# Attention scores of one 256-row batch element: one block-diagonal product per tile before, one product per head after

## The reference, cut to what matters

```
x = x + tanh(g_xattn) * xattn(layernorm(x), ctx)
x = x + tanh(g_ffn)   * ffn(layernorm(x))

xattn:  q = rms_norm(q_in @ Wq per head, qn_w)      # 4 heads of 64
        k = rms_norm((ctx @ Wkv)[k part] per head, kn_w);  v = the other part
        scores = einsum('bqhd,bkhd->bhqk', q, k) / 8       # 256 x 77 for each head
        out = softmax(scores) @ v;  out @ Wfc + fc_b
ffn:    top 2 of 8 experts per row, softmax of the two logits, capacity 97 of a batch element's 256 x 2 places,
        sum over the two kept experts of weight * (x @ We[e])
```

## Time and profile before

| | |
|---|---|
| median of three runs | 1390.62 us |
| profiled execution, first to last instruction (span) | 1388.5 us |
| TensorE matmuls busy | 1364.6 us, 98% of the span |
| TensorE weight loads busy | 1137.0 us, 82% |
| VectorE busy | 1046.5 us, 75% |
| ScalarE busy | 913.9 us, 66% |
| GpSimd busy | 775.2 us, 56% |

### The profile page before, as it was taken

The page is one execution under the profiler, slowest core; times in us unless marked ns, Lnnn a source line. Parts: engine busy times, 40 slices in busy tenths (PEclk is TensorE's granted clock), DMA queues, the critical chain, the costliest instruction groups (busy, mean ns, idle before and its releaser), DMA issues. The chain is left out here.

```text
span 1388.5 us, 26883 instructions
## 1 busy us (share of the span) xinstructions
PE 1364.6 (98%) x8116; PEld 1137.0 (82%) x8116; DVE 1046.5 (75%) x3057; ACT 913.9 (66%) x2600; POOL 775.2 (56%) x947
## 2 busy tenths in 40 slices
PE   7899999999999999999999999999999999999998
PEld 6688888888888888888888888888888888888876
DVE  6877877777877777877778777778777788777763
ACT  6776666775666766667766667666677666676652
POOL 4355555656555656555555566565555555555644
PEclk9999999999999999999999999999999999999999
DMA  5001101011111011110111010111110110101000
GB/s 164 30 18 46 45 28 45 18 45 45 37 37 45 18 46 45 32 42 25 38 45 45 29 45 18 45 45 36 38 39 24 45 45 31 43 18 46 25 16 23
DMA packets 70289, 53.72 MB, mean 39 GB/s; under 512 B 45888, under 2 KB 53504, under 8 KB 70144
## 3 DMA queue, kind: packets, MB, share of 16 engines
q1 hardware_dynamic: 70144, 52.00, 12.1%
HBM read 25.11 MB, written 16.78 MB: 30 GB/s over the span
## 5 line engine op out<-in xcount | busy, mean ns | idle before, releaser
L332 PE MATMUL bkM<-we,x2T 128*128 128x512 f32 x3072 | 791.7, 400 | 0.8 <-DVE acc_v L1067 0.7
L332 PEld LDWEIGHTS bkM<-we,x2T 128*128 128x128 f32 x3072 | 553.6, 188 | 127.6 <-ACT a_out L684 8.4
L684 ACT ACTIVATE a_out<-bkM,gate 128x256 f32<-128x256 f32 x512 | 217.0, 482 | 161.1 <-PE bkM L332 159.9
L1067 DVE SCALAR_TENSOR_TENSOR acc_v<-bkM,gate,acc_v 128x256 f32<-128x256 f32 x384 | 184.8, 481 | 106.2 <-PE bkM L332 91.3
L498 POOL TENSOR_TENSOR a_sum<-a_sum,a_out 128x256 f32<-128x256 f32 x256 | 188.9, 738 | 56.8 <-ACT a_out L684 20.5
L485 POOL TENSOR_TENSOR probs<-probs,p_inv 128x308 f32<-128x308 f32 x128 | 89.8, 702 | 211.6 <-DVE p_inv L960 211.6
L453 POOL TENSOR_TENSOR rstd<-ve,minus_half 128x4 f32<-128x4 f32 x64 | 65.2, 1019 | 145.6 <-DVE ve L872 145.4
L453 POOL TENSOR_TENSOR q_r<-q_ve,minus_half 128x8 f32<-128x8 f32 x64 | 105.0, 1642 | 48.6 <-DVE q_ve L945 48.6
L590 ACT ACTIVATE xn<-x_sb,shift,rstd 128x256 f32<-128x256 f32 x128 | 66.5, 590 | 92.4 <-DVE shift L881 92.4
L453 POOL TENSOR_TENSOR k_r<-k_ve,minus_half 77x8 f32<-77x8 f32 x32 | 52.4, 1637 | 126.9 <-DVE k_ve L921 126.9
L503 POOL TENSOR_TENSOR y<-a_sum,acc_v 128x256 f32<-128x256 f32 x128 | 94.4, 738 | 17.3 <-issue 0.4
(11 more groups left out here) (178 smaller groups left out, 2714.7 us busy)
## 6 DMA issues: line engine op xcount, KB each, us to landing
x_sb<-in_x SPq DMA_DIRECT2D x32, 512.0 KB, 3.7
out<-y SPq DMA_DIRECT2D x64, 256.0 KB, 2.0
ctx_sb<-in_ctx SPq DMA_DIRECT2D x32, 154.0 KB
vf<-v_nat SPq DMA_DIRECT2D x64, 77.0 KB
stage<-in_L_ffn_We SPq DMA_DIRECT2D x2, 1024.0 KB, 7.1
vf<-v_nat SPq DMA_DIRECT2D x32, 52.0 KB
vf<-v_nat SPq DMA_DIRECT2D x32, 51.0 KB
vf<-v_nat SPq DMA_DIRECT2D x32, 26.0 KB
```

The costliest lines, as they stand in the source:

```text
L332: mm = nc.tensor.matmul(out, l, r, start=(i == 0), stop=(i == len(terms) - 1))
L684: ins = nc.scalar.activation(a_out[:, t % 2, (e // 4) * 2 + i], bkM[1][:, i * D:(i + 1) * D], ACT.Copy, scale=gate[:, m.parity, t, e:e + 1])
L1067: nc.vector.scalar_tensor_tensor(out=acc_v[:, t], in0=bkM[0][:, i * D:(i + 1) * D], scalar=gate[:, m.parity, t, e:e + 1], in1=src, op0=ALU ...
```

## The change

`scores` issues four products per tile instead of two, one for each head, each with 64 rows of dimensions and 77 columns of keys: even heads with rows 0 to 63, odd heads with rows 64 to 127. The even heads of both tiles of a batch element go to one bank and the odd heads to another (`head_scores`; `s_bank` is now A, D, B, E). The half of `kd` that holds zeros is no longer read. As each bank now holds heads of two tiles, `row_max` is done once for a batch element: two reductions, one for each bank, then one multiplication for both tiles. `exps` of both tiles wait for it. `p_transpose` overwrites a bank that holds scores of both tiles, so it now waits for the exponentials of both. Scores of tile 1 move from slot 9 to slot 8, and in the second round ahead of `logits`; `row_max` of the second batch element stands in slot 9.

```diff
-        s_bank = [bkA, bkB, bkD, bkE]
+        s_bank = [bkA, bkD, bkB, bkE]
...
-        s_max_done = sig("s_max_done", T)
-        s_bias_done = sig("s_bias_done", T)
+        s_max_done = sig("s_max_done", 2 * BP)
+        s_bias_done = sig("s_bias_done", BP)
...
+        def head_scores(t, j):
+            cols = t % SUB * 2 * LK
+            return s_bank[t // SUB * SUB + j][:, cols:cols + 2 * LK].rearrange("p (m k) -> p m k", m=KC)
...
             def exps(f, t):
-                act.wait_ge(s_bias_done.sem, s_bias_done.at(f, t + 1))
+                act.wait_ge(s_bias_done.sem, s_bias_done.at(f, t // SUB + 1))
...
-                                               s_bank[t][:, h * LK:(h + 1) * LK], ACT.Exp,
+                                               head_scores(t, h % 2)[:, h // 2], ACT.Exp,
...
-            def row_max(f, t):
-                dve.wait_ge(s_ps.sem, s_ps.at(f, t + 1))
+            def row_max(f, b):
+                dve.wait_ge(s_ps.sem, s_ps.at(f, SUB * (b + 1)))
                 dve.wait_ge(exp_done.sem, exp_done.before(f))
-                nc.vector.tensor_reduce(s_max[:, t], s_bank[t][:, 0:HK].rearrange("p (h k) -> p h k", k=LK),
-                                        AX.X, ALU.max).then_inc(s_max_done.sem, 1)
-                dve.wait_ge(s_max_done.sem, s_max_done.at(f, t + 1))
-                dve.wait_ge(q_r_done.sem, q_r_done.at(f, t // SUB + 1))
-                nc.vector.scalar_tensor_tensor(out=s_bias[:, t], in0=s_max[:, t], scalar=-1.0, in1=q_r[:, t],
+                ts = slice(b * SUB, (b + 1) * SUB)
+                for j in range(2):
+                    nc.vector.tensor_reduce(
+                        s_max[:, ts].rearrange("p t (m j) -> p j t m", j=2)[:, j],
+                        s_bank[b * SUB + j][:, 0:SUB * 2 * LK].rearrange("p (t m k) -> p t m k", t=SUB, m=KC),
+                        AX.X, ALU.max).then_inc(s_max_done.sem, 1)
+                dve.wait_ge(s_max_done.sem, s_max_done.at(f, 2 * (b + 1)))
+                dve.wait_ge(q_r_done.sem, q_r_done.at(f, b + 1))
+                nc.vector.scalar_tensor_tensor(out=s_bias[:, ts], in0=s_max[:, ts], scalar=-1.0, in1=q_r[:, ts],
                                                op0=ALU.mult, op1=ALU.mult).then_inc(s_bias_done.sem, 1)
... slot 9 of VectorE: row_max(f, 0), route(p, 0), row_max(f, 1), inverse(f, 0); no row_max in slot 10
             def scores(f, t):
                 pe.wait_ge(kd_done.sem, kd_done.at(f))
-                pe.wait_ge(qT_done.sem, qT_done.at(f, 1 if t == 0 else SUB))
+                pe.wait_ge(qT_done.sem, qT_done.at(f, t // SUB + 1))
                 for m in range(KC):
-                    mm = pe.matmul(s_bank[t][:, m * 2 * LK:(m + 1) * 2 * LK], qT[:, m, t * P:(t + 1) * P],
-                                   kd[:, t // SUB, m].rearrange("p j k -> p (j k)"), start=True, stop=True)
+                    for j in range(2):
+                        h = slice(j * DH, (j + 1) * DH)
+                        mm = pe.matmul(head_scores(t, j)[:, m], qT[h, m, t * P:(t + 1) * P], kd[h, t // SUB, m, j],
+                                       start=True, stop=True)
                 mm.then_inc(s_ps.sem, 1)

             def p_transpose(f, t):
                 pe.wait_ge(probs_done.sem, probs_done.at(f, t + 1))
+                pe.wait_ge(exp_done.sem, exp_done.at(f, t // SUB * SUB + SUB))
... slot 8 of TensorE: scores(f, 0), scores(f, 1), logits_transpose(p); slot 9: scores(f, 2), scores(f, 3)
... second_round: scores(f, 0), scores(f, 1), logits(p), scores(f, 2), scores(f, 3); row_max(f, 1) in place of row_max 1 to 3
```

More of the change, by code:

```diff
@@ L1126, in slot @@
                         row_max(f, 1)
-                        row_max(f, 2)
                         inverse(f, 0)
@@ L1131, in slot @@
                     if f:
-                        row_max(f, 3)
                         inverse(f, 1)
@@ L1202, in second_round @@
                 expert_lo(1, 3)
-                for t in range(1, T):
-                    row_max(f, t)
+                row_max(f, 1)
                 inverse(f, 0)
@@ L1403, in slot @@
                         scores(f, 0)
+                        scores(f, 1)
                     if p:
@@ L1406, in slot @@
                 if k == 9 and f:
-                    scores(f, 1)
                     scores(f, 2)
@@ L1476, in second_round @@
                 scores(f, 0)
+                scores(f, 1)
                 logits(p)
-                for t in range(1, T):
+                for t in range(SUB, T):
                     scores(f, t)
```

## The result

The changed kernel takes 1401.77 us (median of four runs, 1400.26 to 1402.32), the kernel before, run beside it, 1390.62 (median of four runs): 1.0076 times as long, 95% interval 1.0062 to 1.0090. The profiled execution spans 1398.5 us, 10.0 more than before.

What follows compares the result with a forecast made beforehand. TensorE's order was taken as the bound, with chunk 15 waiting on ScalarE's chain without slack. Span 1388.5 plus 18.3 (0.61 x 30 steps) and 1.2 (fill) gave 1408.0, with 2.1 median over span 1410 us; range 1401 to 1453.

Steps and rivals of the forecast that it cites:

- rival A: Changing the number of rows on TensorE costs nothing; ScalarE's chain shifts 0.41 us a step: 1404 us, chance 0.20.
- The direction and its cause: Slower, chance 0.91: ScalarE's chain makes chunk 15 start 0.61 us later a step, TensorE itself arriving only 0.16 later.
- the sign: TensorE's weight-load wait for ScalarE's `a_out` was to rise from 8.4 us by some 10 to 15 us.
- Part 1: Score products on TensorE: two half-row pairs share a 0.11 us slot, 1.76 us a step, 0.33 less than before.
- Rival B: Score loads go one after another, so TensorE decides: 1452 us, or 1433 without change costs; chance 0.30.
- rival C: Halves overlap fully at 0.067 us and ScalarE's chain isn't rigid: TensorE saves 1.02 us a step, 1358 us; chance 0.05.
- Part 2: Changing the number of rows on TensorE: three more changes a step at 0.20 us each, 0.6 us a step.
- The sum on TensorE: Products (-0.33) and changes of the number of rows (+0.60) together: +0.27 us a step on TensorE.
- Part 3: Row maxima ahead of ScalarE's exponentials: scores arrive 0.22 us later, second reduction adds 0.39, so chunk 15 starts 0.61 later.
- What costs nothing: Work on VectorE and later waits claimed free, including the last normalisation with about 0.5 us before its transpose, both shifted alike.
- The sum: 0.61 x 30 steps = 18.3 us plus 1.2 for the fill: span 1408.0, time 1410 us.
- the fill: The two pairs of the fill have the same ScalarE chain, charged 0.6 us each, 1.2 us.

Runs made afterwards that it cites:

- x3: Changed kernel with the scores of all four tiles together in slot 8: 1404.68 us, 1.0093 times the kernel before.
- x4: Changed kernel, ScalarE taking chunk 13 out of PSUM after two of tile 2's four exponentials: 1383.88 us, 0.9944 times the kernel before.
- x7: Changed kernel without the second reduction of a batch element (odd heads' maxima stay zero): 1390.15 us, 0.9993 times the kernel before.
- x1: Changed kernel, each head's product reading all 128 rows, still 77 columns, so no change of row count: 1422.94 us, 1.0226 times the kernel before.
- x10: Kernel before, GpSimd's three additions of ScalarE experts' parts cut to 8 of 256 columns for one tile in four: 1380.32 us, 0.9920.
- x6: Kernel before, ScalarE taking chunk 13 out of PSUM after three of tile 2's four exponentials: 1376.94 us, 0.9898.
- x8: Kernel before, VectorE taking tile 3's reciprocals ahead of chunk 14 in slot 12: 1398.14 us, 1.0047.
- x2: Changed kernel, a tile's four products ordered even, even, odd, odd instead of alternating: 1402.24 us, 1.0076 times the kernel before.

## Why the prediction was right, point by point

The way, the chain and its cause were right, and the range held, but only just: 1401.77 us against a lower end of 1401. The forecast's own 1410 is 8 us too high, a loss of 19 us for the 11 measured, and rival A's 1404, whose mechanism is out, lies nearer. So the time alone tells little, and that it stayed in the range is luck: 5 us came back at a wait that the working did not have, and 0.03 us a step more would have taken it out.

**The direction and its cause** were right: ScalarE's chain sets chunk 15 (x3, x4, x7; the load's wait for `a_out` rose from 8.4 to 17.8 us, where 10 to 15 more were named as the sign), and TensorE's part of the change, +0.20 a step from chunk 10 to chunk 12 (5.63 against 5.43 us), doesn't set the time.

**Part 1**, 1.76 us a step for the products with halves side by side: 16 slots of 0.112 are 1.79. Rival B, loads one after another, and rival C's full overlap at 0.067 are both out; x1 is what B would have been without its change cost, and its 0.11 a load is the 0.105 estimated from three durations. The reason given for 1.76, that the halves have only the load path in common, doesn't fit: two loads, one for each half, start together (729.89) and last 0.18 us, no longer than a load alone (0.19 in the earlier trace rows), so each half is paced by its own loads.

**Part 2**, a drain at each change of rows: the mechanism is right, rival A (none) is out, the size was 0.20 and is 0.15 (x1) to 0.17 (x3). The gap behind the last column is 0.09 as expected, but the first pair costs only 0.06 more (its matmuls are 0.17 ahead of the second pair's, the next ones 0.11), not 0.11. The idle time of the loads put to issue is 0.37 before the scores, for about 0.2, and doesn't stand before chunks 11 and 12, where it was expected too. The sum on TensorE was forecast at +0.27 and is +0.20.

**Part 3**, the shift of ScalarE's chain: 0.61 forecast, 0.54 measured. The second reduction is the 0.39 of the forecast (731.06 to 731.45); what was oversized is the arrival of the scores, +0.14 for +0.22, which has the smaller price of part 2 in it (up to 0.05).

**What costs nothing** is where the forecast missed the largest amount: "the last normalisation has about 0.5 us before its transpose, both shifted alike". TensorE had a second wait in each step, before the attention products, which the working did not take up, put to "issue" in the list of waits (14.6 us in 30 times, 8.8 after). It hung on VectorE's gate arithmetic, which hung on GpSimd. With chunk 15 late, VectorE had finished chunk 14 and the routing earlier relative to it, the last normalisation on GpSimd started 0.2 earlier, `den` was held 0.49 us instead of 0.68, and 0.17 a step came back. x10 shortens this wait through GpSimd alone, and x6 and x8 move it; that these steps make up the chain in the changed kernel itself is read from its trace, and no run there isolates it.

**The sum.** Of the 9.5 us between the forecast span (+19.5) and the measured (+10.0), 0.08 x 30 = 2.4 are the chain's size, 0.19 x 30 = 5.7 the part given back, and 1.2 the fill, which had been charged and lost nothing.

## What to carry to other kernels

A TensorE that is 98% busy can still be paced by another engine: look for the wait that occurs once in each step, however small, and for the chain in front of it. What lengthens that chain is paid at that wait (0.39 us taken out of it gave 11.6 us, x7), though a later wait can give part of it back; what shortens TensorE ahead of it is waited away (x3). Moving one take-out of PSUM ahead of the last of four exponentials was worth 14 us here (x6), where the half-row products by themselves have shown no gain in time. They run side by side, but each entry and exit costs TensorE 0.15 to 0.17 us, so they are cheaper for it in one group (5.29 us for 5.63).

## What the runs showed of the hardware

- Loads and matmuls on rows 0 to 63 and on rows 64 to 127, to different banks, run in pairs up to 0.01 us apart, and a load of 128 columns paces each half at 0.11 us; with a tile's odd heads' products queued behind its even ones the pairs remain (x2), so the two halves' matmuls start in another order than the program's.
- A change between 128 and 64 rows costs TensorE 0.15 us (x1) to 0.17 us (x3).
- A VectorE instruction on four float32 numbers a row took 0.16 us free and 0.68 us behind a GpSimd instruction; cutting GpSimd's additions for one tile in four short took 11 us from the kernel without another change (x10).
